# A three-layer graph kernel: one turning product, zero-mean weights in two layers, and new orders for the first steps

## The reference

```python
u = einsum('bid,bjd->bij', h, h) / sqrt(384)
attn = softmax(u) * adj;  attn = attn / (attn.sum(-1) + 1e-10)
ctx = (attn above diagonal) @ (h @ Wl.T + bl) + diag(attn) * (h @ Ws.T + bs) \
    + (attn below diagonal) @ (h @ Wr.T + br)
out = relu((ctx - mean(ctx)) / sqrt(var(ctx) + 1e-12) * gamma + beta)
```

## Time and profile before

| | before |
|---|---|
| median of three runs | 1231.8 us (1230.98 to 1233.81) |
| the profiled execution | 1233.29 us |
| its span | 1231.5 us |
| granted PE clock over the span | 0.996 |
| PE busy | 1215.2 us (99%), 7163 instructions |
| PE weight loads busy | 1208.6 us (98%) |
| DVE busy | 1089.2 us (88%), 3127 instructions |
| ACT busy | 833.1 us (68%), 2079 instructions |
| POOL busy | 326.8 us (27%), 439 instructions |
| DMA | 127.18 MB, mean 103 GB/s |

### The profile page before, as it was taken

One profiled execution on the slowest core, in us unless ns is written; L12 is line 12 of the kernel. 1 busy time (PEld: TensorE's weight loads), 2 busy tenths in 40 slices (PEclk: granted clock), 3 DMA queues, 4 the chain that ended last, 5 costly groups with the idle time before them and its releaser, 6 DMA issues.

```text
span 1231.5 us, 26747 instructions
## 1 busy us (share of the span) xinstructions
PE 1215.2 (99%) x7163; PEld 1208.6 (98%) x7163; DVE 1089.2 (88%) x3127; ACT 833.1 (68%) x2079; POOL 326.8 (27%) x439
## 2 busy tenths in 40 slices
PE   7899999999999999999999999999999999999997
PEld 6899999999999999999999999999999999999997
DVE  6799888888887799999999999999999999999986
ACT  6577767666666667776766666676666666676764
POOL 1234232222222123321212121232323232323221
PEclk9999999999999999999999999999999999999999
DMA  5444232324232234333333323322332323232321
GB/s 179 135 121 129 89 114 83 118 82 119 83 106 91 94 99 130 116 100 104 96 106 96 107 85 103 129 85 95 97 107 98 106 95 99 96 97 98 99 91 54
DMA packets 112922, 127.18 MB, mean 103 GB/s; under 512 B 11104, under 2 KB 100192, under 8 KB 112864
## 3 DMA queue, kind: packets, MB, share of 16 engines
q1 hardware_dynamic: 112864, 126.50, 32.8%
HBM read 76.91 MB, written 49.55 MB: 103 GB/s over the span
## 4 chain that ended last, share of the span: by engine, by line
PE 97%; DMA 1%; issue 1%; DVE 1%; SPq 0%; ACT 0%; POOLq 0%; POOL 0%; DVEq 0%; ACTq 0%
PE right_bank L448 25%; PE left_bank L448 24%; PE context_bank L448 24%; PE context_bank L479 17%; PE score_bank L423 6%; PE score_bank L431 1%; DMA rows<-weights 1%; DMA nodes<-squares 0%; PE edge_bank L438 0%; ACT side_parts L610 0%; DVE context L872 0%; SPq L340 0%; DVE rows L881 0%; DVE stats L844 0%; DVE turned L744 0%
## 5 line engine op out<-in xcount | busy, mean ns | idle before, releaser
L448 PE MATMUL left_bank<-weight,node_t 128*128 128x384 f32 x1728 | 338.1, 339 | 0.0
L448 PE MATMUL right_bank<-weight,node_t 128*128 128x384 f32 x1728 | 335.0, 338 | 2.2 <-DVE weight L827 2.2
L448 PE MATMUL context_bank<-weight,node_t 128*128 128x384 f32 x1728 | 332.3, 337 | 3.1 <-ACT context_bank L616 3.1
L610 ACT ACTIVATE side_parts<-right_bank 128x384 fp32r<-128x384 f32 x192 | 94.4, 492 | 317.3 <-PE context_bank L479 317.1
L448 PEld LDWEIGHTS context_bank<-weight,node_t 128*128 128x128 f32 x1728 | 303.0, 188 | 3.7 <-ACT context_bank L616 3.4
L448 PEld LDWEIGHTS left_bank<-weight,node_t 128*128 128x128 f32 x1728 | 304.3, 188 | 0.0
L448 PEld LDWEIGHTS right_bank<-weight,node_t 128*128 128x128 f32 x1728 | 299.4, 188 | 3.5 <-issue 2.6
L479 PE MATMUL context_bank<-side_parts,attn_t 128*128 128x386 f32 x1152 | 240.0, 344 | 2.2 <-issue 1.9
L479 PEld LDWEIGHTS context_bank<-side_parts,attn_t 128*128 128x128 f32 x1152 | 198.9, 189 | 4.5 <-issue 3.6
L748 DVE TENSOR_TENSOR node_t<-nodes,node_t 128x768 fp32r<-128x768 f32 x94 | 121.6, 1294 | 18.2 <-ACT node_t L558 18.2
L1034 POOL TENSOR_TENSOR edge_block<-edge,tri 128x512 f32<-128x512 f32 x96 | 131.9, 1374 | 0.0
(11 more groups left out here) (78 smaller groups left out, 1519.6 us busy)
## 6 DMA issues: line engine op xcount, KB each, us to landing
squares<-turned SPq DMA_DIRECT2D x94, 384.0 KB, 2.7
nodes<-squares SPq DMA_DIRECT2D x376, 96.0 KB, 2.2
rows<-x SPq DMA_DIRECT2D x64, 384.0 KB, 3.7
out<-rows SPq DMA_DIRECT2D x31, 384.0 KB, 2.6
adj_in<-adj SPq DMA_DIRECT2D x96, 64.0 KB, 1.9
piece<-weights SPq DMA_DIRECT2D x18, 192.0 KB, 2.5
rows<-weights SPq DMA_DIRECT2D x3, 576.0 KB, 8.5
vector_rows<-vectors SPq DMA_DIRECT2D x3, 384.0 KB, 5.3
```

Source lines behind the costliest of these rows:

```text
L448: mm = nc.tensor.matmul(bank[:, 0:D], node_t[:, s.parity, k, c, a], weight[:, s.phase % 2, w, c, b], start=False, stop=(c, a) == (CH - 1, ...
L610: nc.scalar.activation(side_parts[:, side, HI, 0:D], side_bank[side][k][:, 0:D], ACT.Copy).then_inc(side_hi[side], 1)
```

## The change

1. **Turning.** ACT packs the cross blocks that lie off the diagonal of both tiles side by side, in four copies, and one product into the free columns of edge_bank turns them. DVE adds the plain cross term in two instructions on 64 partitions as before, now as soon as the copies are there (`sum_scores`), and the turned one in a third (`add_cross`).
2. **Zero-mean weights** in phases 1 and 2. ACT takes the mean of each row of a weight piece over the outputs (`average_piece`) and subtracts it in the split of the next step; DVE, no longer POOL, makes the rest. Bias rows are levelled the same way (`level_bias`). The context then has mean zero: for all steps but the last, `context_stats` and `gather_moments` go, ACT squares and sums the context instead (`square`), and `centre` only multiplies by gamma.
3. **Pieces** come one every second step from step 3 on, and 22 steps of phases 0 and 1 are written out (2 of phase 2). Bias rows of the next phase are loaded in step 8 instead of 29.
4. **Orders.** `seed_side(s,1,RIGHT)` moves to the head of ACT's step; in phase 1 the shift moves ahead of a residual; the sums move ahead of the input statistics; the first two steps get orders of their own on PE, ACT and DVE.
5. **Loads at the start** are shared between SP and ACT's queue; the first tile comes in two halves, the first chunk of the right weights by itself, and the first projection waits for tile 0 alone.

```diff
-PIECES_IN = {3: 2, 4: 2, 5: 2, 6: 2, 7: 1}
+PIECES_IN = {3 + 2 * i: 1 for i in range(PIECES)}
+WRITTEN = 11
+BIAS_IN = {PAIRS - 4: RIGHT, PAIRS - 3: LEFT, PAIRS - 2: SELF}
+    def level(self):
+        return self.phase > 0 and self.ahead(1).exists()
...
+        cross_blocks = cross[:, :, :].rearrange("p a (b j) -> p (a b) j", b=2)
+        cross_pack = cross_blocks[:, 1:3].rearrange("p b j -> p (b j)")
+        cross_here = [cross_blocks[half, 1 - h:4 - h:2] for h, half in enumerate(HALVES)]
+        turned_cross = edge_bank[:, 3 * P:4 * P].rearrange("p (k j) -> p k j", k=2)
```

On PE:

```diff
             def turn_cross(s):
-                pe.wait_ge(cross_copied, s.n + 1)
-                for k in range(2):
-                    mm = nc.tensor.matmul(score_bank[:, k * 256:k * 256 + P], cross[:, k], ident_r[:, :],
-                                          start=False, stop=True, skip_group_check=True)
-                mm.then_inc(cross_turned, 1)
+                pe.wait_ge(cross_packed, 4 * (s.n + 1))
+                at_least(pe, cross_added, s.n)
+                nc.tensor.matmul(edge_bank[:, 3 * P:4 * P], cross_pack, ident_r[:, :],
+                                 start=True, stop=True, skip_group_check=True).then_inc(cross_turned, 1)
+            def second_step(s):
+                prev, nxt = s.ahead(-1), s.ahead(1)
+                project_side(s, 0, RIGHT)
+                weigh(prev, 1)
+                project_side(s, 0, LEFT)
+                project_self(s, 0)
+                project_side(s, 1, RIGHT)
+                project_side(s, 1, LEFT)
+                scores(nxt)
+                weigh(s, 0)
+                project_self(s, 1, within=lambda: turn_cross(nxt))
...
-            keep_busy(3)
+            keep_busy(5)
...
-            keep_busy(6)
+            keep_busy(5)
```

On ACT; the second step has the body's operations with `split_nodes(nxt)` and `copy_cross(nxt)` after `seed_self(s, 1)`:

```diff
             def copy_cross(s):
                 act.wait_ge(scored, s.n + 1)
+                at_least(act, cross_turned, s.n)
                 at_least(act, score_summed, 2 * s.n)
-                nc.scalar.activation(cross[:, :, :], scores4[:, :, 1, :], ACT.Copy).then_inc(cross_copied, 1)
+                for h, half in enumerate(HALVES):
+                    nc.scalar.activation(cross_here[h], scores4[half, :, 1, half], ACT.Copy).then_inc(cross_packed, 1)
+                for h, half in enumerate(HALVES):
+                    nc.scalar.activation(cross_blocks[HALVES[1 - h], 1 + h], scores4[half, 1 - h, 1, half], ACT.Copy).then_inc(cross_packed, 1)
...
+            def average_piece(phase, i):
+                n = (phase - 1) * PIECES + i
+                act.wait_ge(piece_in[n % 2], 16 * (n // 2 + 1))
+                nc.scalar.activation(piece_part(phase, i, HI), piece[:, n % 2], ACT.Copy, scale=-1.0 / D,
+                                     accum_out=piece_mean[:, n % 2:n % 2 + 1]).then_inc(piece_averaged, 1)
+            def square(s, k):
+                act.wait_ge(centred, s.tile(k) + 1)
+                act.wait_ge(spread_done, s.n)
+                nc.scalar.activation(context_bank[k][:, 0:D], context_bank[k][:, 0:D], ACT.Square, scale=float(D) ** -0.5,
+                                     accum_out=moments[:, k, 1:2]).then_inc(squared, 1)
```

ACT's `first_step`:

```diff
                 split_edges(s)
-                fill_source(second, 0)
-                fill_source(second, 1)
                 scale_self(s, 0)
                 seed_self(s, 1)
                 copy_cross(nxt)
                 seed_side(nxt, 0, RIGHT)
+                fill_source(second, 0)
+                fill_source(second, 1)
                 split_side(s, 1, RIGHT)
                 split_side(s, 1, LEFT)
-                fill_source(third, 0)
-                fill_source(third, 1)
                 scale_self(s, 1)
                 seed_side(nxt, 0, LEFT)
                 exponentials(nxt)
+                fill_source(third, 0)
+                fill_source(third, 1)
```

ACT's `body`, and its loads ahead of the first step:

```diff
                 if nxt.exists():
                     split_nodes(nxt)
+                if prev.exists() and prev.level():
+                    square(prev, 0)
+                seed_side(s, 1, RIGHT)
                 split_side(s, 0, RIGHT)
...
-                seed_side(s, 1, RIGHT)
                 scale_self(s, 0)
                 if nxt.exists():
                     copy_cross(nxt)
                 seed_side(s, 1, LEFT)
+                if prev.exists() and prev.level():
+                    square(prev, 1)
                 if len(pieces) > 0:
-                    split_piece(*pieces[0])
+                    average_piece(*pieces[0])
+                if len(averaged) > 0:
+                    split_piece(*averaged[0])
+                if bias_of(s) is not None:
+                    level_bias(s.phase + 1, bias_of(s))
...
+            act.dma_start(rows[:, 1], x_pairs[0, :, 1]).then_inc(x_in[0], 16)
+            load_first(RIGHT, (0,), first_chunk_in)
+            load_first_bias(RIGHT)
+            load_first(RIGHT, (1, 2), first_in[RIGHT])
+            load_first(LEFT, (0, 1, 2), first_in[LEFT])
+            load_first_bias(LEFT)
```

On DVE:

```diff
+            def add_cross(s):
+                dve.wait_ge(cross_turned, s.n + 1)
+                dve.wait_ge(score_summed, 2 * s.n + 2)
+                nc.vector.tensor_tensor(score[:, :, :], score[:, :, :], turned_cross, ALU.add).then_inc(cross_added, 1)
```

More of the change, by code:

```diff
@@ L111, in pieces_of, with bias_of @@
     return [(s.phase + 1, first + i) for i in range(PIECES_IN[s.g])]
+def bias_of(s):
+    if not isinstance(s.n, int) or s.phase + 1 == PHASES or s.g not in BIAS_IN:
+        return None
+    return BIAS_IN[s.g]
 def walk(eng, body):
@@ L117, in walk @@
         first, last = phase * PAIRS // 2, (phase + 1) * PAIRS // 2 - 1
-        for half in range(first, first + 4):
+        written = WRITTEN if phase + 1 < PHASES else 1
+        for half in range(first, first + written):
             body(Step(phase, half, 0))
             body(Step(phase, half, 1))
-        with eng.Fori(first + 4, last - 1) as half:
+        with eng.Fori(first + written, last - 1) as half:
             body(Step(phase, half, 0))
@@ L626, in split_piece @@
                 n = (phase - 1) * PIECES + i
-                act.wait_ge(piece_in[n % 2], 16 * (n // 2 + 1))
-                nc.scalar.activation(piece_part(phase, i, HI), piece[:, n % 2], ACT.Copy).then_inc(piece_hi, 1)
-            def split_first(w):
-                act.wait_ge(first_in[w], 16)
-                for i in range(w * CH, (w + 1) * CH):
-                    nc.scalar.activation(piece_part(0, i, HI), first_raw[:, i], ACT.Copy).then_inc(first_hi[w], 1)
+                act.wait_ge(piece_averaged, n + 1)
@@ new lines, in split_piece, with level_bias @@
+                nc.scalar.activation(piece_part(phase, i, HI), piece[:, n % 2], ACT.Identity,
+                                     bias=piece_mean[:, n % 2:n % 2 + 1]).then_inc(piece_hi, 1)
+            def level_bias(phase, w):
+                n = 3 * (phase - 1) + list(BIAS_IN.values()).index(w)
+                act.wait_ge(bias_rows_in[phase % 2], 16)
+                at_least(act, piece_lo, phase * PIECES)
+                nc.scalar.activation(piece[:, n % 2], vector_row(phase, ROW_LEFT + w), ACT.Copy, scale=-1.0 / D,
+                                     accum_out=bias_mean[:, w:w + 1]).then_inc(bias_averaged, 1)
+                act.wait_ge(bias_averaged, n + 1)
+                nc.scalar.activation(vector_row(phase, ROW_LEFT + w), vector_row(phase, ROW_LEFT + w), ACT.Identity,
+                                     bias=bias_mean[:, w:w + 1]).then_inc(bias_levelled, 1)
@@ new lines, in square, with split_first @@
+            def square(s, k):
[3 more added lines that the diff above has]
+                                     accum_out=moments[:, k, 1:2]).then_inc(squared, 1)
+            def split_first(w, chunks=range(CH)):
+                for i in chunks:
+                    act.wait_ge(first_chunk_in if (w, i) == (RIGHT, 0) else first_in[w], 16)
+                    nc.scalar.activation(piece_part(0, w * CH + i, HI), first_raw[:, w * CH + i], ACT.Copy).then_inc(first_hi[w], 1)
@@ L926, in body @@
                 split_side(s, 0, RIGHT)
-                if prev.exists():
+                if prev.exists() and not prev.level():
                     gather_moments(prev, 1)
@@ L930, in body @@
                     spreads(prev)
+                if s.phase == 2 and fourth.exists() and fourth.bounded:
+                    input_stats(fourth, 0)
+                    input_stats(fourth, 1)
                 if third.exists():
@@ L946, in body @@
                     place_max(nxt)
+                if prev.exists() and prev.level():
+                    spreads(prev)
                 if fourth.exists() and fourth.bounded:
@@ L972, in body @@
                     return
-                centre(s, 0)
+                if not s.level():
+                    centre(s, 0)
                 if nxt.exists() and not nxt.bounded:
```

235 lines of the change are left out of this document (171 added, 64 removed).

## The result

The changed kernel takes **1234.45 us** (median of 12 runs, 1233.26 to 1236.77), the kernel before 1231.74 (12 runs, 1230.62 to 1233.81). The ratio is 1.0021, interval 1.0012 to 1.0030: slower by 2.7 us, where 12.6 us less were forecast. The profiled execution has a span of 1233.3 us at a mean granted clock of 0.991.

The account below looks back on a forecast made before the run. The prediction took TensorE (PE), 97% of the chain, to bound the kernel. Its terms, -11.0 - 0.8 + 0.2 - 1.0 = -12.6 us, gave 1219.2 us from a median of 1231.8, with a range of 1214 to 1224.

Parts of the forecast that it names:

- the term for the start: Loads and first steps: old waits partly go, later node reads bring a new one; -1.0 us, between +3 and -6.
- the wait of about 3 us in step 2: Step 2: node reads go out about 43, landing late; a 3 us wait replaces the 3.44 in step 1.
- two waits of 3 us: Start: the case behind the upper end of the start's range, +3 us.
- Turning product, -11.0: PE, every step: one turning product instead of two saves 0.11 to 0.12 us, 96 times; -11.0 us.
- The other estimate, 7.8 us: PE: the turning term by the skill page's figure of about 81 ns for a product of 128 columns.
- The copies: ACT before the turn: four copies take 0.79 us; PE pays nothing while they take under 0.95.
- rival (c): PE before the turn: the four copies are late, 0.27 us a step at the upper end, 1245 us; chance 0.05.
- DVE's order in phase 1, cost 0: DVE, phase 1: last left split ends at 8.7 against a need of 8.82; cost 0, upper end 0.3 a step.
- ACT's squares, cost 0: ACT, phases 1 and 2: two squares, about 0.6 us each, fit its idle gaps; 10.2 of 12.4 us, cost 0.
- rival (d): ACT: Square needs another table than the exponentials, four loads a step, 1400 us; chance 0.03.
- The stalls, -0.8 and +0.2: Phase 1: 0.19 us in four steps goes, -0.8; near its end old stalls go, new ones come, +0.2.
- 0.86 for faster: Whole kernel: the summed chance that the changed kernel is faster, against 0.06 within and 0.08 slower.

Follow-up runs that it names:

- e4: The changed kernel with the loads and first two steps of the kernel before; one turning product and zero-mean weights stay: 1221.87 us, ratio 0.9924.
- e1: The changed kernel with DVE's input shift for step 5 moved to the end of its second step: 1228.57 us, ratio 0.9977.
- h1: e1 with that input's statistics behind the masked edges, and POOL placing those edges ahead of the input's root: 1227.22 us, ratio 0.9962.
- g1: e4 with a mended order of the second step: fill and node split earlier, input 5's shift in step 2, POOL's edges first: 1219.56 us.
- g2: g1 with ACT's and DVE's splits of the nodes moved further ahead, and ACT's fill with its split: 1217.06 us, ratio 0.9877.
- e3: e4 with the changed kernel's loads: two queues, their new order, first right chunk alone, 5 and 5 products on zeros: 1225.39 us, ratio 0.9952.
- f1: e4 with the one turning product of each step issued twice: 1232.83 us, ratio 1.0008.
- f3: e4 with a fifth 64x64 copy on ACT, read by nobody, ahead of the last two copies: 1225.97 us, ratio 0.9953.
- f2: e4 with zero-mean weights kept but unused: mean and variance by DVE's statistics, no square on ACT: 1239.49 us, ratio 1.0057.

## Why the prediction was wrong, and where it was right

**The failed step is the term for the start: -1.0, between +3 and -6; it was +13.8 in the trace, and 12.6 us by the medians of the changed kernel and e4.** The mechanism was wrong there, not only the size. Three things in it.

- *The moved fills.* The prediction counted that the squares behind the fill go out later and named the wait of about 3 us in step 2. That wait came (4.51, with the reads at 56.03, not 43). It didn't ask who else waits for the fill. POOL's root does, since its buffer is single; and the new order puts DVE's shift, which waits for that root, ahead of the sums of the next step. With the shift alone put out of the way 5.9 us come back (e1). No rival had it, and the upper bound of two waits of 3 us left it out.
- *The own order of DVE in step 1.* Its statistics of input 5 stand ahead of the split of nodes. That an input landing at 41.8 now guards the scores of step 2 was not looked at. What it is worth alone isn't settled: 1.35 us with the fills as they are (h1). The mended order of step 1, with fills and splits forward, takes 2.3 us (g1) and 4.8 us (g2) less than e4, so an own order for that step was worth having; this one was not.
- *The loads.* Forecast: left weights 1.7 us later, and the left projection no earlier, at no cost in the sum. They landed 1.95 us later (14.88 against 12.93), and the new loads cost 3.5 us (e3). The landing was right and its price was not. The self weights, wanted last, now landed at 12.33 (16.14 before), ahead of the left ones. The rest is a term that the prediction didn't have: the left bias, issued ahead of the left weights before, is now issued behind them and landed at 15.85. ACT stood at the seed that needs it and started the split of the left weights only at 16.90, 2.0 us behind their landing; before it was at 13.10, 0.2 behind. So of the 3.8 us between these splits about half is the later landing of the weights and half what ACT still had to do behind the late bias, the seed and a fill. This is read from the times; no run has the second queue with the bias first. The Trainium skill (DMA: Bandwidth & Descriptors, Issuing engines are not separate DMA queues) says that copies of different engines share the same 16 DMA engines and only issue time is saved. The result agrees: over the first 16 us both kernels moved 261 GB/s, at a DMA share of 0.82 before and 0.83 after.

Right, point by point:

- **Turning product, -11.0.** f1 gives 11.0 by the medians, 10.7 from step 4 on. Steps of 12.35, 12.48, 12.37 were forecast; 12.347, 12.467 and 12.347 came. The other estimate, 7.8 us, worked out from the 81 ns that the Trainium skill (TensorE: Matmul & The Clock Gate, Back-to-back issue gap) gives for 128 columns, is refuted for this stream: one such product is worth 0.12 to 0.13 us here.
- **The copies.** Cost 0 was right, by luck: two sizes were wrong and cancelled. The four take 1.06 us, not 0.79. In phases 0 and 1 they start 1.08 us after the scores, not 1.16, and end 0.15 ahead of the turn (timeline of the changed kernel, phase 1):

```profile
623.04 0.83 PEld L442 LDWEIGHTS score_bank<-node_t 128*128 128x128 f32 x6
...
624.12 0.57 ACT L606 ACTIVATE cross<-score_bank 64x128 fp32r<-64x128 f32 x2
624.72 0.46 ACT L608 ACTIVATE cross<-score_bank 64x64 fp32r<-64x64 f32 x2
...
625.33 0.19 PEld L450 LDWEIGHTS edge_bank<-ident_r,cross 128*128 128x128 f32 x1
```

  By the prediction PE waits from 0.95 us on. In phase 2 the copies did start at 1.16 and end at 2.21, and by the 0.18 counted for the signal PE should have waited about 0.1 us a step. It didn't, since the signal took 0.04 at most (f3). The cover left is 0.04 us in phase 2 and about 0.11 in the others, so rival (c) was nearer than the chance of 0.05 says.
- **DVE's order in phase 1, cost 0.** The last left split ended 8.53 us after the scores, 8.7 forecast, need 8.82. In f2 PE starts 0.12 us after the end of that split, so the cover is 0.29 less about 0.12. f2 also shows what the 1 us less of statistics was worth in this order: 0.46 a step.

```profile
631.02 0.55 DVE L968 TENSOR_TENSOR side_parts<-left_bank,side_parts 128x384 fp32r<-128x384 f32 x1
```

- **ACT's squares, cost 0; the table, rival (d).** ACT has 10.88 us in a phase 1 step, forecast 10.2, and no product waits. The table was loaded once: Square needed no other here.
- **The stalls, -0.8 and +0.2.** The stall in four steps is gone. Near the end of phase 1 three steps take 13.00 us, 0.53 each over 12.47, 0.6 to 0.7 forecast. The stall is split between the spread product and the weighing, and the first part was not named:

```profile
789.96 0.19 PEld L456 LDWEIGHTS edge_bank<-max_diag,same_graph 128*128 128x128 f32 x1 [0.32 <-DVE max_diag L900]
794.51 0.48 PEld L500 LDWEIGHTS context_bank<-side_parts,attn_t 128*128 128x128 f32 x3 [0.31 <-issue]
```

The chances, 0.86 for faster, took the start's range as a bound it wasn't: its upper end was made of the waits that had been found. What stays open: how the 13.8 us divide between waits and the slow clock that follows them; how the 3.5 us divide between the second queue and the order of the loads; the 0.7 of the first step's order, which lies within the spread; and the 2.7 us by which even e4 lies above the forecast.

## What to carry to other kernels

When an instruction is moved later, follow everything that waits for it, the reuse of a buffer that it reads among it, and then what stands behind those waiters on their in-order engines; here a 0.16 us shift held an engine for 6.95 us. An instruction for work four steps ahead belongs behind all that the next step needs, even if it is short. A gain on the bounding engine is safe to sum over the steps, but only as long as the cover is measured: here 0.04 to 0.11 us under the copies and 0.2 to 0.3 on DVE. And look at what a part of the change that is priced at 0 protects: without the use of the zero-mean weights phase 1 lost 0.46 us a step (f2). When loads are given a new order, look also at the small ones: here a bias row behind the weights held ACT, and by the times of the rows that was half of what the left projection lost.

## What the runs showed that was not expected

- A copy on ACT from a PSUM bank costs little less for fewer partitions and elements: 0.38 us for one of 128x256, 0.57 for two of 64x128, 0.46 for two of 64x64. The four parts took 1.06 us, nearly three times the whole, for fewer elements.
- Loads shared between two issuing engines, in a new order, landed the weights wanted second 1.95 us later and made the kernel 3.5 us slower, with the same bytes to move and the same 261 GB/s over the first 16 us.
- A copy that is shown as 0.22 us long moved the end of the copies behind it by only 0.12 us: on an engine whose instructions overlap, an added one is priced by the starts, not by its shown length.
- The first scores' start varied by 1.7 us (12.75 to 14.47) between kernels with the same loads, while steady steps repeat within 0.02 us. Between g1 and g2 the 1.1 us is the clock: nine projections took 2.74 us at 0.50 granted, and 1.53 at 1.00.
